# A small GpSimd fill between any two indirect DMAs of five kinds of stage in a graph network kernel

## The reference, cut to what matters

```
agg = segment_sum(h[src], dst) / deg                      # SAGE, three times
mean_agg = segment_sum(h[s0], d0) / max(cnt, 1)           # end of the GAT block ("mean")
for i in range(4):                                        # JK, four times
    h = relu(segment_sum((h * norm_src)[src], dst) * norm_dst @ Ws[i] + bs[i])
    h = relu(batchnorm(h));  xs.append(h)
out = segment_sum(norm * (h @ W)[row], col) + b           # GCN, three times
```

## Time and profile before

| what | value |
|---|---|
| median of 3 runs | 6739.2 us (6734.26 to 6741.9) |
| profiled execution, first to last instruction | 7555.6 us |
| instructions in it | 86,623 |
| GpSimd busy | 3999.0 us, 53% of the span |
| TensorE, VectorE, ScalarE busy | 4855.1, 4654.8, 3050.2 us |
| DMA moved | 1292.14 MB |

### The profile page before, as it was taken

How to read it: one execution, slowest core, us unless ns; L and a number is a source line. 1 busy time by engine, 2 the same in 40 slices (tenths; PEclk the granted TensorE clock), 3 DMA queues, 4 the chain that set the end, 5 groups by cost and what they waited for, 6 DMA issues and landing times. The chain is left out here.

```text
span 7555.6 us, 86623 instructions
## 1 busy us (share of the span) xinstructions
PE 4855.1 (64%) x23532; PEld 3254.8 (43%) x23532; DVE 4654.8 (62%) x13695; ACT 3050.2 (40%) x6979; POOL 3999.0 (53%) x3991
## 2 busy tenths in 40 slices
PE   6888888779978625686233443434899995579211
PEld 4666665445558403575222222211555553346111
DVE  4777666223358627668674455656899995644444
ACT  3555554443334103344343333333677773245000
POOL 4565553544435466556555565656333334654766
PEclk9999999889989755796555666766899997789555
DMA  6988665776768423696343475754677675565232
GB/s 143 226 240 231 209 206 188 215 215 226 243 201 245 121 45 92 187 257 185 109 122 103 124 118 110 128 96 88 234 248 256 244 251 156 173 183 177 84 88 73
DMA packets 1104141, 1292.14 MB, mean 171 GB/s; under 512 B 133903, under 2 KB 815679, under 8 KB 1097390
## 3 DMA queue, kind: packets, MB, share of 16 engines
q1 hardware_dynamic: 973518, 1032.63, 43.5%
q0 software_dynamic: 130144, 253.97, 16.5%
HBM read 607.93 MB, written 682.10 MB: 171 GB/s over the span
## 5 line engine op out<-in xcount | busy, mean ns | idle before, releaser
L570 POOL DMA_INDIRECT jk_layer_msg<-jk,idx_jk x588 | 593.7, 1010 | 376.5 <-issue 173.4
L1057 PE MATMUL jk_layer_sum_ps<-ident,jk_layer_weighted 128*128 128x128 f32 x784 | 178.9, 369 | 733.6 <-ACT jk_layer_weighted L1023 382.1
L2084 POOL TENSOR_TENSOR rows_moved<-rows_x_in,w_lonely_row 128x512 f32<-128x512 f32 x98 | 124.6, 1272 | 677.3 <-DVE rows_x L671 640.9
L1057 PEld LDWEIGHTS jk_layer_sum_ps<-ident,jk_layer_weighted 128*128 128x128 f32 x784 | 114.6, 183 | 844.8 <-ACT jk_layer_weighted L1023 431.5
L1079 DVE TENSOR_TENSOR_SCAN jk_layer_sum_t<-goes_on,jk_layer_sum_t,jk_layer_sum_ps 128x512 f32<-128x512 uint8 x196 | 250.1, 1276 | 346.3 <-DMA sage_nodes_x_in<-in_x 288.0
L1886 ACT ACTIVATE jk_layer_h_t<-jk_layer_h_ps,w_jk_b 128x512 f32<-128x512 f32 x196 | 134.7, 687 | 631.8 <-DMA gat_own<-yv 337.9
L696 PE MATMUL sage_nodes_h_ps<-sage_nodes_h_t,w_ws 128*128 128x512 f32 x784 | 353.6, 594 | 0.0
L1198 DVE COPY sage_h<-sage_turn 128x512 f32<-128x512 f32 x98 | 67.8, 692 | 456.7 <-PE sage_turn L687 348.3
L894 ACT ACTIVATE sage_nodes_h_t<-sage_nodes_h_ps,w_b_c 128x512 f32<-128x512 f32 x392 | 248.9, 688 | 239.8 <-PE sage_nodes_h_ps L696 114.8
L696 PE MATMUL sage_h_ps<-sage_sum_t,w_wn 128*128 128x512 f32 x588 | 296.7, 614 | 59.0 <-issue 58.8
L2283 PE MATMUL gcn_end_sum_ps<-ident,gcn_end_rows 128*128 128x128 f32 x196 | 54.7, 434 | 426.9 <-DVE gcn_end_rows L2276 215.4
(11 more groups left out here) (454 smaller groups left out, 16299.8 us busy)
## 6 DMA issues: line engine op xcount, KB each, us to landing
h<-sage_nodes_h SPq DMA_DIRECT2D x196, 512.0 KB
h_t<-sage_h_t SPq DMA_DIRECT2D x98, 512.0 KB
h<-sage_h SPq DMA_DIRECT2D x98, 512.0 KB
jk_t<-jk_layer_h_t SPq DMA_DIRECT2D x196, 256.0 KB
rows_layers<-jk_t SPq DMA_DIRECT2D x49, 1024.0 KB, 5.9
r<-rows_h SPq DMA_DIRECT2D x98, 512.0 KB
second_x_in<-u SPq DMA_DIRECT2D x147, 260.0 KB
jk<-jk_layer_h SPq DMA_DIRECT2D x147, 256.0 KB
```

Source lines behind the costliest of these rows:

```text
L570: pool.indirect_dma_start(out=into[:, g.number % depth, s, :], out_offset=None, in_=table, in_offset=bass.IndirectOffsetOnAxis(ap=index_ti ...
L1057: mm = pe.transpose(ps[:, c, at_s], self.weighted[:, g.b, s, c * P:(c + 1) * P], self.K.ident[:])
L2084: pool.tensor_tensor(moved[:, g.b], x_in[:, g.number % 3], to_subs(W.lonely_row), ALU.add).then_inc(lonely_added.sem, 1)
```

## The change

A class `Spacer` owns a tile of 4 x 256 bytes per partition and a semaphore. `pool_space` issues one `memset` on GpSimd that fills a quarter of it (128 x 256 uint8). Every fourth fill adds one to the semaphore, and ahead of every fourth fill (from the fifth on) GpSimd waits for the fourth of the round before. Such a fill is put behind each indirect DMA of the five kinds of stage: 196 in `fetch`, 196 in `mean`, 4 x 196 in `jk`, 196 in `gcn_first`, and 392 in `gcn_end` (gather and scatter). These are 1764 fills. Nobody reads the tile.

```diff
+SPACE = 256
...
-def pool_gather(pool, g, index_tile, used, table, into, arrived):
+class Spacer:
+    def __init__(self, ph):
+        self.tile, self.filled, self.n = ph.sb("space", [P, SUB, SPACE], U8), ph.sem("space_filled"), 0
+
+    def pool_space(self, pool):
+        turn, s = divmod(self.n, SUB)
+        if s == 0 and turn:
+            pool.wait_ge(self.filled, turn)
+        ins = pool.memset(self.tile[:, s, :], 0)
+        if s == SUB - 1:
+            ins.then_inc(self.filled, 1)
+        self.n += 1
+
+def pool_gather(pool, g, index_tile, used, table, into, arrived, spacer=None):
...
     for s in range(SUB):
         pool.indirect_dma_start(out=into[:, g.number % depth, s, :], ...).then_inc(arrived.of(g), 16)
+        if spacer is not None:
+            spacer.pool_space(pool)
...
 # fetch_block
         for t in range(ET):
             pool.indirect_dma_start(out=kept[:, t, :], ...).then_inc(arrived[t % 4], 16)
+            spacer.pool_space(pool)
...
 # SegmentSums
+        self.spacer = Spacer(ph) if width == D and index is not None else None
...
 # LoopSums
+        self.spacer = Spacer(ph) if width == D else None
...
 # gcn_end_block, scatter
                 pool.indirect_dma_start(out=out_dram, ...).then_inc(scattered.of(g), 16)
+                sums.spacer.pool_space(pool)
```

More of the change, by code:

```diff
@@ L577, in fetch_block @@
     arrived = [ph.sem(f"arrived{b}") for b in range(4)]
-    counts = SourceCounts(ph, K, counts_table)
+    counts, spacer = SourceCounts(ph, K, counts_table), Spacer(ph)
     block = ph.block()
@@ L1007, in pool_fetch @@
     def pool_fetch(self, pool, g):
-        pool_gather(pool, g, self.index, self.used, self.table, self.msg, self.arrived)
+        pool_gather(pool, g, self.index, self.used, self.table, self.msg, self.arrived, self.spacer)
     def sync_messages(self, sp, g):
@@ L2265, in pool_fetch @@
     def pool_fetch(self, pool, g):
-        pool_gather(pool, g, self.K.idx, self.joined, self.table, self.msg, self.arrived)
+        pool_gather(pool, g, self.K.idx, self.joined, self.table, self.msg, self.arrived, self.spacer)
     def sync_own(self, sp, g):
```

## The result

| kernel | median of 4 runs | range | ratio, 95% interval |
|---|---|---|---|
| before | 6736.73 us | 6731.51 to 6741.9 | 1 |
| changed | 7084.66 us | 7075.12 to 7091.36 | 1.0527 [1.0512, 1.0541] |

The fills make the kernel 348 us slower, 0.197 us for each of the 1764. The prediction was 7020 us, in a range of 6620 to 7120.

What follows compares the result with a forecast made beforehand. The prediction took GpSimd's instruction list to bound the eight stages in timed runs, near 1.25 us per DMA. 1764 fills at 0.17 us make 300, less 20 for cover in `mean`: 6739.2 + 280 = 7020 us, range 6620 to 7120.

Steps and rivals of the forecast that it cites:

- The reading of the waits: Stalls of VectorE and GpSimd in the profiled stages come from the recording falling behind; some 410 of 816.4 us excess.
- Rivals one and two: One: waits real and stay, only `gcn_end` pays, 6762 to 6790, chance 0.13. Two: fills thin them, 6627, chance 0.25.
- all of them near 1.25 us per DMA: In timed runs GpSimd's list sets the length of the eight stages, at about 1.25 us per indirect DMA.
- d: Length of one 256-byte fill between two indirect DMAs, taken as 0.25 us; price 0.17 us per DMA.
- two small terms: Around each fill: it starts 0.02 us after the DMA ends, and the next DMA takes 0.99 instead of 0.95.
- rival three: The fill is cheap at all 1764 places: 0.12 us long, +0.04 us per DMA, 71 us, 6810; chance 0.09.
- The waits on the fill before: Every fourth fill waits for the one before, already done: costs nothing; up to 0.1 us per DMA if reported late.
- No cover in `fetch`, JK, the first GCN stage and `gcn_end`: Other engines hide none of the fills there; `gcn_end`, at 67 us, is the largest single item.
- the sum: All fills: 1764 x 0.17 = 300 us, less 20 us, gives 280 us; `gcn_end` is 392 x 0.17 = 67 us.
- Cover in `mean`: VectorE at 5.03 us per group, level with GpSimd's 5.01, may hide part of the fills: 20 us off.

Runs made afterwards that it cites:

- second profile of the kernel before: The kernel before, unedited, timed and profiled again: 6718.59 us against 6715.05 (1.0007), span 6717.8 us.

## Why the prediction held, and where it was off

**The reading of the waits.** The prediction held that the stalls of VectorE and GpSimd are in the profile and not in the timed runs, and named as its test a median up by 250 or more beside a span up by less than 100. The median rose by 348 and the span fell by 473. The repeated profiles settle that much: GpSimd's idle time in them is the gap between its own instructions (59.4 us over 195 in `fetch`, `mean` and the first JK layer), and the stages are as long as the list and what stands ahead of its first and behind its last DMA. Rivals one and two both needed the waits to be in the timed runs. The first would have given 6762 to 6790, the second 6627.

That the recording fell behind is not shown. The first profile's excess stands only in stages with indirect DMAs, and no run separates a recording that held the engines up there from something else that slowed this one execution; nothing in the kernel tells the two apart. The forecast needed only that the timed runs are without it. The prediction expected the changed kernel's profile to lag too ("about 7600"), and it did not. It also leaned on an instruction "whose only input it had itself made"; L1764 reads `mean_x_in` as well, which had come by DMA, but L1762 had read the same tile 3.87 us earlier, so it was there, and the point stands. And "all of them near 1.25 us per DMA" was too short for some stages: it is 1.35 beside the count, and the DMAs of the later JK layers take 1.01 us on average, not 0.95.

**The fill.** This is the term that was mis-sized. d was taken at 0.25 us, from the spacing of two memsets of 256 elements; it is 0.33, two hundredths above the duration in the same rows, 0.31, which was the upper end of the range. In the earlier trace rows one memset starts 0.06 us before the other ends; between two DMAs nothing overlaps the fill. Against that, two small terms went the other way: the DMA behind a fill takes 0.95, not the 0.99 of the earlier trace rows, which is the length of that kind of DMA (`src_count`, 0.98 on average) and not an effect of what stands ahead of it; and the fill's start 0.02 late does not show. The price then is 0.95 + 0.33 + 0.16 - 1.25 = 0.19 us, where 0.17 was predicted; 1764 x 0.19 = 335 of the 348 us. By elements and not by bytes was right, as the 64-element fill shows, and rival three (d = 0.12) fell with it.

The Trainium skill's "GPSIMD Engine Reference", section "Performance versus the Vector engine", gives 1.03 cycles per element for the simplest loops, from which the prediction had its estimate of 0.22 us for 256 elements. The slope that the fills show (0.83 ns per element) agrees with that rate at 1.2 GHz (0.86 ns); what the estimate leaves out is the fixed 0.12 us, which the earlier trace rows had. The two added would have given 0.34. The Trainium skill's "Perfetto Trace Analysis", section "DMA Instruction — SWDGE (GPSIMD)", has the DSP end such a DMA only after the end that is recorded; from this the prediction worked out 441 us, for a fill that adds its whole length. The one-byte fill decides against that sum for this kernel: 5 us for 1764 instructions of 0.12 to 0.14 us, so the gap does take up what stands in it, to 0.14 us.

**The waits on the fill before.** Costed at nothing, and so it is: GpSimd stands still for 0.5 us in all ahead of 784 fills in JK, and the one-byte kernel has the same waits.

**No cover in `fetch`, JK, the first GCN stage and `gcn_end`.** Right, and `gcn_end` came out as predicted: 67 us by the sum, 66.2 by the stage's length, 76 (67 to 87) by itself. `fetch` pays 31.6 us, somewhat less than 196 x 0.19 = 37: beside the count the interval grows from 1.35 to 1.48 us only, because the DMAs there took 1.05 us without a fill and take 0.95 with one.

**Cover in `mean`.** Wrong: 20 us were taken off, and the stage pays 39.0 in the profile and 39 by itself. The prediction held VectorE level with GpSimd, at 5.03 us per group against 5.01, and took half of the fills' price off in case GpSimd were quicker in timed runs. Level it is, but GpSimd is not quicker: in the second profile of the kernel before VectorE is busy for 213 of 220 us in the middle of the stage and waits for TensorE four times in all:

```profile
DVE mean_sum_t L1079 <- PE mean_sum_ps L1057: 15.0, 4, 11.0
```

In the changed kernel it waits in nearly every group, and two scans lie 5.95 apart:

```profile
3359.16 1.28 DVE L1100 TENSOR_TENSOR_SCAN mean_sum_t<-goes_on,mean_sum_t,mean_sum_ps 128x512 f32<-128x512 uint8 x1 [0.62 <-PE mean_sum_ps L1078]
...
3365.11 1.28 DVE L1100 TENSOR_TENSOR_SCAN mean_sum_t<-goes_on,mean_sum_t,mean_sum_ps 128x512 f32<-128x512 uint8 x1 [0.79 <-PE mean_sum_ps L1078]
```

Who waits for whom in the same stage of the changed kernel (us in total, times, longest):

```profile
ACT mean_weighted L1044 <- DMA mean_msg<-yv,idx_y: 69.4, 48, 10.7
...
DVE mean_sum_t L1100 <- PE mean_sum_ps L1078: 49.5, 48, 11.3
POOL mean_msg L587 <- issue: 32.1, 195, 0.3
```

With four fills GpSimd needs some 5.8 us per group and VectorE still 5.03, so the stage goes by GpSimd. An engine that is level with the bound gives no cover: what is added to the bound is added to the stage. VectorE would have covered only by as much as it took longer than GpSimd.

**What the sum had no term for.** The DMAs of the later JK layers take 1082 ns behind fills in place of 1010 (588 x 0.07 = 42 us), those of the first GCN stage 1010 in place of 959 (10 us). With fills in those stages alone it is the same, 1088 and 1009 ns. So it belongs to the stage's own work, and since the 512-element fill leaves them at 1019 and 951, it is not the fill that lengthens them but the moment at which the DMA falls. A piece of the changed kernel's JK timeline, GpSimd's rows and one of VectorE's:

```profile
4299.40 1.04 POOL L587 DMA_INDIRECT jk_layer_msg<-jk,idx_jk  x1 [0.17 <-issue]
...
4300.45 0.33 POOL L575 MEMSET jk_layer_space<- 128x256 uint8 x1
...
4300.94 1.34 POOL L587 DMA_INDIRECT jk_layer_msg<-jk,idx_jk  x1 [0.16 <-issue]
...
4301.49 0.69 DVE L1940 SCALAR_TENSOR_TENSOR jk_layer_square<-jk_layer_off 128x512 f32<-128x512 f32 x1
...
4302.28 0.33 POOL L575 MEMSET jk_layer_space<- 128x256 uint8 x1
4302.77 0.95 POOL L587 DMA_INDIRECT jk_layer_msg<-jk,idx_jk  x1 [0.16 <-issue]
```

Sorted over all 588 DMAs of these layers, the long ones are those that lie beside this VectorE instruction: 137 of them take 1.33 us on average, the other 451 take 1.01, and 137 x 0.32 = 44 us covers the whole of the 42. In the first GCN stage it is the 48 beside VectorE's scan, 1.18 against 0.96. The instruction alone does not do it: in the second profile of the kernel before the DMAs beside `jk_layer_square` took 1.01 like the rest, and with 512-element fills 1.02 like the rest. So it hangs on how the two lists fall beside each other, and why a DMA is held up in one such position and not in another stays open. That VectorE's work can hold these DMAs up fits `fetch`, where in the kernel before they take 1.05 us while the count runs and 0.95 once it is over.

About 45 us come back elsewhere: by shorter waits ahead of the JK layers (72.9 to 59.7) and for the scatter's norm (12.7 to none), and by DMAs that got shorter, in the scatter (1079 to 1023 ns, 11 us) and in `fetch` (8 us). So the forecast, 68 us short, owes part of its nearness to terms that cancel: against the 280 us predicted stand 35 more for the fill, 20 for the cover in `mean` and 52 for the longer DMAs, and 45 less for these.

## What to carry to other kernels

Before costing an edit from a profile, compare its span with the timed median; if they differ by more than the runs do among themselves, profile the unchanged kernel again, and read no wait from the first. Work that is put into the list of the engine that bounds a stage costs its whole length less the gap that it takes up, and an engine that merely keeps pace with it covers nothing; the same work is nearly free where the engine waits for another. Take a short instruction's cost as its duration with the fixed part in it, not as the spacing of two of them.

## What the runs showed of the hardware that was not expected

- A memset on GpSimd of 128 partitions takes 0.12 us and 0.83 ns per element of a partition, whatever the element's size: 64 int32 took 0.17, 256 uint8 0.33, though both are 256 bytes.
- Between two indirect DMAs GpSimd stands still for 0.30 us, but for 0.16 behind a memset, which itself is recorded to start as the DMA ends. An instruction of up to 0.14 us there is all but free: 1764 of them cost 5 us (3 to 15).
- An indirect DMA of 128 rows took 0.95 us alone and 1.05 beside the one-hot count, in the same stage and the same list. The count is held up in turn: VectorE's second one-hot instruction (L529 of the kernel before) takes 0.24 us on average without fills, 0.33 with 256-element fills and 0.43 with 512, and the count as a whole 132, 144 and 165 us. It moves in step with GpSimd, two columns to each of GpSimd's intervals of 1.35, 1.48 and 1.69 us.
- One profile of the kernel before lasted 816.4 us longer than its timed runs, with each engine's busy time within about 2% of that of the next profile. The extra time stood as waits with plausible names in the stages with indirect DMAs alone; two more profiles lasted as long as the runs.
